# An LSTM recurrence run over 125 lanes in four rounds: a shorter 16-bit rough round, one two-pass round that keeps its sums and states, two rounds of changes, and another order of TensorE's work

## The chip, the cores and the metric

The kernel runs on one core of a Trainium2 chip. The metric is the device time of one execution in microseconds (us).

## The reference, cut to what matters

x has 6250 rows of 512. First a graph layer (a sum over 100,000 edges, two dense layers), then an LSTM over the 6250 rows as one sequence, each with a residual:

```python
x = x + gnn(layernorm(x), edge_index, W1, b1, W2, b2)
def step(carry, x_t):                      # 6250 steps, h and c of 512
    combined = concatenate((x_t, h_prev))
    f_t = sigmoid(combined @ W_f + b_f);  i_t = sigmoid(combined @ W_i + b_i)
    c_tilde = tanh(combined @ W_c + b_c); o_t = sigmoid(combined @ W_o + b_o)
    c_t = f_t * c_prev + i_t * c_tilde;   h_t = o_t * tanh(c_t)
x = x + lstm(layernorm(x), W_f, b_f, W_i, b_i, W_c, b_c, W_o, b_o)
```

## The kernel before, in words

table_part and graph_part compute the graph layer, the rows x1 and, for each of them, the 2048 gate inputs (gate_rows, in DRAM). lstm_part then does the recurrence. It cuts the sequence of 6250 into 125 lanes (L) of 50 steps (STEPS) and runs all lanes side by side, one lane to a partition. A lane's starting state is unknown at first, so it runs in rounds: after each, measure turns the ends of the lanes (cell, product of the forget gates, output gate) by TensorE into columns and takes the gap between a lane's end and the next lane's start, and correct makes new starts from the gaps by a scan with the products (decay). Before, the rounds are rough and close (one pass of rounded weights each), full (three passes: W_high and W_low with the state, W_high with the state's low part; it stores the sums of the gates in total_rows and the turned states in h_steps, both in DRAM) and delta (one pass of W_high with the difference between the new state and the stored one, on top of the stored sums). After full the gaps must be under LOOSE, after delta under TOLERANCE; otherwise rounds "more" (three passes) follow.

The four accumulators acc[n] are one PSUM bank each of 512 columns: n = 0 forget and input gates of the first 256 units, 1 cell and output gates of them, 2 and 3 the same of the second 256 units. product(n, k) is one matmul of 512 columns with the state chunk k (FIRST is k = 0, 1, SECOND is k = 2, 3), 16 in a pass. turn transposes h chunk by chunk into hturn (PSUM); take_turned or moved makes the state of it, and new products wait for it. The rows of a step come by DMA into xg, four buffers deep; they enter the accumulator by a matmul with the identity (add_rows), by a copy into PSUM ahead of the products (seed; seeded is TensorE's wait for it), or, in full, by VectorE's add_inputs into total. Each engine takes its instructions in the order that step writes down for it, and nothing else: in delta, ScalarE has forget_input(0), cell_gate(0), output_gate(0), forget_input(1), new_cell(FIRST) (tanh), cell_gate(1), seed(0), seed(1), output_gate(1), new_cell(SECOND), seed(2), seed(3).

## Time and profile before

| | |
|---|---|
| median of 3 runs | 3029.12 us (3022.49 to 3034.47) |
| profiled execution, span | 3303.4 us; no time of its own is given beside the span |
| granted TensorE clock, mean | 0.938 |
| TensorE busy | 2872.7 us, 87% |
| VectorE busy | 2206.3 us, 67% |
| ScalarE busy | 1745.7 us, 53% |
| GpSimd busy | 996.9 us, 30% |
| DMA | 648.45 MB, 196 GB/s |

The rows shown ahead of the prediction give times from the start of the span. PE is TensorE's matmuls, PEld its weight loads, DVE is VectorE, ACT is ScalarE, POOL is GpSimd. Shares of the whole span are means over stages with different limits, so the stages are to be read one by one.

### The profile page before, as it was taken

What the parts mean: (1) busy time and instruction counts of PE and PEld (TensorE: products, weight loads), DVE (VectorE), ACT (ScalarE), POOL (GpSimd) and SP (SyncE); (2) the same over time, 40 slices, a digit from 0 to 9 for tenths busy, and PEclk for the clock granted to TensorE, in tenths of its full rate; (3) what the DMA queues carried; (4) which work ended last, traced back from release to release, by engine and by line L of the source; (5) the groups of instructions that cost most, each with busy time, mean ns of one, the idle gap of its engine ahead of it and who ended that gap; (6) DMA issues with size and microseconds to landing.
All of it is one profiled execution on the core that took longest, in us unless ns stands there. A gap on an engine that the chain in (4) does not pass through costs nothing. (4 is left out here: it accounts for less than half of the span.)

```text
span 3303.4 us, 57302 instructions
## 1 busy us (share of the span) xinstructions
PE 2872.7 (87%) x11844; PEld 2116.3 (64%) x11845; DVE 2206.3 (67%) x5730; ACT 1745.7 (53%) x4557; POOL 996.9 (30%) x1008
## 2 busy tenths in 40 slices
PE   6967887888887988887869999999999999978786
PEld 5846665666665766665656666666677777755554
DVE  6746776767766766665757886666666666666665
ACT  4644444444444444444437776777344444447775
POOL 1135555555555655555540000000000000003332
PEclk9979988999898999988989999999999999989998
DMA  8556767677776777667666665664466656669997
GB/s 221 159 169 197 204 200 205 200 210 207 209 209 205 212 211 203 205 200 211 191 177 184 183 179 150 171 174 136 138 196 193 194 192 194 194 182 269 260 272 185
DMA packets 234635, 648.45 MB, mean 196 GB/s; under 512 B 65914, under 2 KB 87674, under 8 KB 203334
## 3 DMA queue, kind: packets, MB, share of 16 engines
q1 hardware_dynamic: 161768, 410.64, 42.8%
q0 software_dynamic: 72816, 237.24, 25.1%
q8 instruction: 19, 0.31, 0.0%
q14 instruction: 32, 0.26, 0.0%
HBM read 493.56 MB, written 154.16 MB: 196 GB/s over the span
## 5 line engine op out<-in xcount | busy, mean ns | idle before, releaser
L1474 PE MATMUL acc<-W_high,state 128*125 128x512 f32 x3200 | 998.3, 417 | 43.3 <-ACT acc L1407 38.7
L1474 PEld LDWEIGHTS acc<-W_high,state 128*125 128x125 f32 x3200 | 595.2, 191 | 242.1 <-ACT state L1354 57.1
L785 POOL DMA_INDIRECT rows<-ln_table,slab x400 | 409.5, 1024 | 467.0 <-issue 230.0
L1316 POOL TENSOR_TENSOR out<-h,lx 125x512 f32<-125x512 f32 x50 | 64.2, 1283 | 1394.0 <-DVE h L1753 1394.0
L785 POOL DMA_INDIRECT Wh<-ln_table,slab x400 | 406.1, 1015 | 217.5 <-issue 152.4
L819 ACT ACTIVATE high<-rows 128x512 fp32r<-128x512 f32 x400 | 243.6, 628 | 332.7 <-DMA rows<-ln_table,slab 225.6
L867 PE MATMUL agg<-high,onehot 128*125 128x512 f32 x800 | 347.8, 435 | 52.9 <-DVE low_part L976 38.0
L819 ACT ACTIVATE high<-Wh 128x512 fp32r<-128x512 f32 x400 | 241.3, 629 | 225.2 <-DMA Wh<-ln_table,slab 117.5
L867 PE MATMUL agg<-low_part,onehot 128*125 128x512 f32 x800 | 327.7, 410 | 0.0
L1474 PE MATMUL acc<-W_low,state 128*125 128x512 f32 x800 | 316.3, 395 | 0.0
L1733 DVE TENSOR_TENSOR fc<-gate,c 125x256 f32<-125x256 f32 x400 | 168.7, 422 | 210.4 <-ACT gate L1373 206.5
L976 DVE TENSOR_TENSOR low_part<-rows,high 128x512 fp32r<-128x512 f32 x400 | 261.4, 692 | 70.7 <-ACT high L819 47.3
L976 DVE TENSOR_TENSOR low_part<-Wh,high 128x512 fp32r<-128x512 f32 x400 | 263.9, 690 | 16.3 <-issue 8.0
L1474 PE MATMUL acc<-W_high,h_low 128*125 128x512 f32 x800 | 263.7, 401 | 0.0
L1373 ACT ACTIVATE gate<-acc 125x512 f32<-125x512 f32 x300 | 179.5, 598 | 146.8 <-PE acc L1474 138.7
L1753 DVE TENSOR_TENSOR h<-gate,tc 125x128 f32<-125x128 f32 x800 | 198.5, 288 | 85.6 <-ACT tc L1399 84.9
L1354 ACT ACTIVATE state<-hturn 128x125 fp32r<-128x125 f32 x600 | 140.0, 275 | 187.7 <-PE hturn L1494 181.1
L867 PEld LDWEIGHTS agg<-high,onehot 128*125 128x125 f32 x800 | 157.1, 196 | 123.0 <-issue 52.4
L887 PE MATMUL gps<-Wx_high,zT_high 128*125 128x512 f32 x800 | 221.9, 399 | 14.2 <-ACT zT_high L854 11.9
L913 PE MATMUL late<-W_high,h1T_high 128*125 128x512 f32 x200 | 108.7, 543 | 142.6 <-ACT h1T_high L836 82.5
L1399 ACT ACTIVATE tc<-c 125x128 f32<-125x128 f32 x800 | 203.8, 304 | 53.7 <-DVE c L1745 53.1
L1494 PE MATMUL hturn<-ident,h 125*128 125x125 f32 x800 | 192.2, 295 | 37.3 <-DVE h L1753 37.3
(217 smaller groups left out, 5032.7 us busy)
## 6 DMA issues: line engine op xcount, KB each, us to landing
xg<-gate_rows SPq DMA_DIRECT2D x150, 896.0 KB
gate_rows<-gout SPq DMA_DIRECT2D x200, 224.0 KB
total_rows<-total SPq DMA_DIRECT2D x50, 896.0 KB
xg<-total_rows SPq DMA_DIRECT2D x50, 896.0 KB
xg<-gate_rows SPq DMA_DIRECT2D x150, 104.0 KB
lx<-x_rows POOLq DMA_DIRECT2D x50, 250.0 KB, 8.2
out_dram<-out POOLq DMA_DIRECT2D x50, 250.0 KB, 8.3
h_steps<-hT SPq DMA_DIRECT2D x49, 250.0 KB, 2.6
```

The lines of the kernel that those rows point to most:

```text
L785: e.indirect_dma_start(out=rows[j % RING][:, :], out_offset=None, in_=table[:, :], in_offset=bass.IndirectOffsetOnAxis(ap=slabs[j // SLAB] ...
L819: e.activation(high[j % PARTS][:, :], rows[j % RING][:, :], ACT.Copy).then_inc(s_high, 1)
L867: m = e.matmul(agg[0:L, :], onehot[:, j % HOT_RING, :], part[j % PARTS][:, :], start=(j == 0 and part is high), stop=(part is low_part), s ...
L887: products.append(e.matmul(gps[n][0:L, :], state[:, k, :], weights[:, k, n // 2, n % 2].rearrange("p s c -> p (s c)"), start=(begins and k ...
L976: e.tensor_tensor(low_part[j % PARTS][:, :], rows[j % RING][:, :], high[j % PARTS][:, :].bitcast(F32), ALU.subtract).then_inc(s_low, 1)
L1354: e.activation(state[:, k, :], hturn[k][:, :], ACT.Copy).then_inc(s_state[k], 1)
L1373: e.activation(gate[0:L, half, 0].rearrange("c s u -> c (s u)"), gates, ACT.Sigmoid).then_inc(s_fi[half], 1)
L1399: e.activation(tc[0:L, k], c[0:L, k], ACT.Tanh).then_inc(s_tc[k], 1)
L1474: m = e.matmul(acc[n][0:L, :], stationary[:, k, :], weights[:, k, n // 2, n % 2].rearrange("p s c -> p (s c)"), start=begins, stop=(k == K ...
L1494: e.transpose(hturn[k][:, :], h[par][0:L, k], ident[0:L, 0:L]).then_inc(s_turn[k], 1)
L1733: e.tensor_tensor(fc[0:L, of].rearrange("c k u -> c (k u)"), gate[0:L, half, 0, 0], c[0:L, of].rearrange("c k u -> c (k u)"), ALU.mult).th ...
L1753: e.tensor_tensor(h[par][0:L, k], gate_of(k, 1, 1), tc[0:L, k], ALU.mult).then_inc(s_h[k], 1)
```

## The change

The rounds are now rough, kept, change and final. Rough begins at step SKIP = 12 of each lane (38 steps) with cells, gates and h in 16 bits (fp16, in the memory of total); its turned h is copied into the state by VectorE, no longer ScalarE. Kept has two passes (W_high and W_low with a state that has 16 bits, so there is no low part) and h in 16 bits; its sums go to total_rows as before, its states stay on chip in kept, in the memory in which the weights and some working buffers of the earlier parts were. Change and final are what delta was, against these sums and states, and take their old states from kept instead of a DMA. Only final stores the result. All one-pass rounds share one order of TensorE (one_pass); the seed of accumulator 3 is VectorE's in all of them. fc is gone, the cell is multiplied in place. After kept the gap of the cells counts a quarter, and LOOSE is 2^-3. The diff, cut:

```diff
+SKIP = 12
 TOLERANCE = 2.0 ** -17
-LOOSE = 2.0 ** -7
+LOOSE = 2.0 ** -3
+CELL_SHARE = 0.25
...
+        kept = sb(top, "kept", [P, STEPS, K * LANES], F16)
+        Wh = (kept[:, :, :].rearrange("p t u -> p (t u)")[:, 0:2 * K * G4].bitcast(F32)
+              .rearrange("p (k a b s c) -> p k a b s c", k=K, a=2, b=2, s=2))
+        beside = kept[:, :, :].rearrange("p t u -> p (t u)")[:, 2 * K * G4:].bitcast(I32)
...
+        halves = [t[:, :, :, :].rearrange("p a b g -> p (a b g)").bitcast(F16) for t in total]
+        r_gate = halves[0][:, 0:G4].rearrange("p (a b s u) -> p a b s u", a=2, b=2, s=2)
+        r_c, r_ic, r_tc = (halves[1][:, n * D:(n + 1) * D].rearrange("p (k u) -> p k u", k=K) for n in range(3))
+        r_decay = halves[1][:, 3 * D:4 * D].rearrange("p (a u) -> p a u", a=2)
+        h_half = [t[:, :, :].bitcast(F16)[:, :, 0:P] for t in h]
...
+        hturn = [pb(ctx, f"hturn{k}", [P, P]) for k in range(K)]
+        hturned = [t[:, 0:L] for t in hturn]
+        hturned_half = [t[:, :].bitcast(F16)[:, 0:L] for t in hturn]
...
+        def steps_of_round(e, kind, step):
+
+            begin = SKIP if kind == "rough" else 0
+            step(begin, 0, True, False)
+            with e.Fori(0, (STEPS - 2 - begin) // ROWS) as i:
                 for n in range(ROWS):
-                    step(i * ROWS + (n + 1), (n + 1) % ROWS, False, False)
+                    step(i * ROWS + (begin + n + 1), (n + 1) % ROWS, False, False)
...
+            for r, kind in enumerate(("rough", "kept", "change", "final")):
+                steps(r, kind)
+                measure(r, kind, {"kept": 0, "final": 1}.get(kind))
+                if kind != "final":
+                    correct(r, kind)
...
-            for t in (c, c_start, h_start, gap, h_gap, change):
+            for t in (c, c_start, h_start, gap, h_gap, change, r_c):
                 e.memset(t[:, :, :], 0.0).then_inc(s_clear, 1)
-            e.memset(decay[:, :, :], 1.0).then_inc(s_clear, 1)
+            for t in (decay, r_decay):
...
+                e.memset(t[:, :, :], 1.0).then_inc(s_clear, 1)
+            e.memset(tc_start[:, :, :], 0.0).then_inc(s_clear, 1)
...
                         cell_gate(1)
                         output_gate(1)
+                        new_cell(SECOND)
+                    elif kind == "kept":
+                        if not first:
+                            keep(SECOND, s - 1)
+                        new_cell(FIRST)
+                        forget_input(1)
+                        if not last:
+                            take_turned(FIRST, now)
+                        cell_gate(1)
+                        output_gate(1)
+                        if not last:
+                            keep(FIRST, s)
...
+                    else:
                         forget_input(1)
...
-                        output_gate(1)
-                        if kind == "full" and not last:
-                            keep(FIRST, s, par, summed)
-                    new_cell(SECOND)
-                    if kind == "delta":
+                        new_cell(SECOND)
                         seed(2)
-                        seed(3)
-                    elif last:
-                        take_turned(SECOND, now)
-                steps_of_round(e, step)
+                steps_of_round(e, kind, step)
+                if kind == "kept":
+                    for s in s_state:
+                        e.sem_inc(s, 1)
 
             def correct(r, kind):
                 e.wait_ge(s_cs, r + 1)
@@ -1460,9 +1464,9 @@
         @block.tensor
         def _(e):
             for s in (*s_acc, *s_turn, s_taken):
-                e.sem_inc(s, AHEAD)
...
+                            e.wait_ge(s_seed_v, SEEDED + (s - SKIP))
+                        elif n == 3:
+                            e.wait_ge(s_seed_v, SEEDED + (STEPS - 1 - SKIP) + (r - CHANGE) * (STEPS - 1) + s)
                         else:
...
+                    def one_pass():
+                        if first:
+                            e.wait_ge(s_begin, r + 1)
+                        if first or kind == "rough":
+                            for n in range(4 if first else 3):
+                                m = add_rows(n)
+                            if first:
+                                m.then_inc(s_taken, 1)
+                        if not first:
+                            turn(FIRST, 1 - par, now - 1)
+                        if not first and kind != "rough":
+                            seeded(1)
+                        for n, k in ((0, 0), (1, 0), (0, 1), (1, 1)):
+                            product(n, k)
+                        if kind != "rough":
+                            seeded(2)
+                        for k in FIRST:
+                            product(2, k)
+                        if not first:
+                            turn(SECOND, 1 - par, now - 1)
+                        for n in range(2):
+                            for k in SECOND:
                                 product(n, k)
-
...
                         seeded(3)
...
-                            product(3, k)
-
-                    def close_step():
-                        add_rows(0)
-                        turn(FIRST[:1], 1 - par, now - 1)
-                        add_rows(1)
-                        turn(FIRST[1:], 1 - par, now - 1)
...
+                    def two_passes():
                         if first:
                             e.wait_ge(s_begin, r + 1)
                             e.wait_ge(s_clear, CLEARED + K)
                         for k in FIRST:
                             stated(k)
+                        for n in range(3):
+                            e.wait_ge(s_sum[n], now - 1)
+                            products(n, FIRST, OF_HIGH, True)
+                        if not first:
+                            turn(SECOND, 1 - par, now - 1)
+                        for k in SECOND:
+                            stated(k)
                         for n in range(2):
-                            e.wait_ge(s_sum[n], summed - 1)
+                            products(n, SECOND, OF_HIGH, False).then_inc(s_acc[n], 1)
+                        e.wait_ge(s_sum[3], now - 1)
+                        products(3, FIRST, OF_HIGH, True)
+                        products(2, SECOND, OF_HIGH, False).then_inc(s_acc[2], 1)
+                        products(3, SECOND, OF_HIGH, False).then_inc(s_acc[3], 1)
+                        turn(FIRST, par, now)
...
+                    gates, cell, took, cell_turned, faded = gate, c, ic, tc, decay
+                to_h = h_half if kind in ("rough", "kept") else h
+                if kind == "change":
+                    for k in range(K):
+                        e.wait_ge(s_kept[k], r * STEPS + AHEAD - 1)
+
...
-                            e.tensor_tensor(state[:, k, :], hturn[k][:, :], hT[par][:, k, :],
+                            e.tensor_copy(state[:, k, :], hturned_half[k]).then_inc(s_state[k], 1)
+
+                    def moved(ks):
+                        for k in ks:
+                            e.wait_ge(s_turn[k], now)
+                            e.tensor_tensor(state[:, k, :], hturned[k],
+                                            kept[:, bass.ds(s + 1, 1), k * L:(k + 1) * L]
+                                            .rearrange("p o l -> p (o l)"),
                                             ALU.subtract).then_inc(s_state[k], 1)
...
-                        if kind == "delta" and not last:
-                            moved(FIRST[:1], s, par, now)
+                        if not last:
+                            if kind == "rough":
+                                take_turned(FIRST)
+                            else:
+                                moved(FIRST[:1])
                         for k in SECOND:
                             new_cell(k)
-                        if kind == "delta" and not last:
-                            moved(FIRST[1:], s, par, now)
+                        if not last and kind != "rough":
+                            moved(FIRST[1:])
                         new_h(SECOND)
-                        if kind == "delta":
-                            if not last:
-                                moved(SECOND, s, par, now)
-                        else:
+                        if not last:
+                            if kind == "rough":
+                                take_turned(SECOND)
+                            else:
+                                moved(SECOND)
+                        if kind == "rough":
                             decayed()
-                        if kind == "rough" and not last:
+                        if not last:
                             seed()
+                    elif kind == "kept":
+                        add_inputs(0, landed=True)
+                        add_inputs(1)
+                        forgotten(0)
+                        taken_in(0)
+                        for k in FIRST:
+                            new_cell(k)
+                        add_inputs(2)
+                        new_h(FIRST)
+                        add_inputs(3)
+                        forgotten(1)
+                        taken_in(1)
+                        for k in SECOND:
+                            new_cell(k)
+                        new_h(SECOND)
+                        decayed()
                     else:
                         if not first:
...
+                turned = ends_half if kind == "rough" else ends
...
+                if kind == "rough":
+                    e.wait_ge(s_clear, CLEARED + K)
+                    after_own(e.tensor_copy(begun, h_start[:, :, :]))
+                    after_own(e.tensor_copy(state[:, :, :], begun))
+                elif kind in ("kept", "change"):
+                    after_own(e.tensor_tensor(state[:, :, :], h_start[:, :, :], begun, ALU.subtract))
```

## Rows read from the trace of the kernel before

**Rows 1.** The page: span of the profiled execution

```profile
span 3303.4 us, 57302 instructions
```

**Rows 2.** Windows from each round's first sigmoid: length, busy time of the engines, clock, DMA

```profile
0.00:1714.60 1714.60, 1407.71 (x5831) 1076.79 (x5832) 1148.37 (x2374) 781.50 (x1513) 869.50 (x856) 0.91 0.69 201
1714.60:2021.60 307.00, 291.74 (x1171) 193.67 (x1170) 240.22 (x710) 212.67 (x702) 11.25 (x5) 0.96 0.63 173
2021.60:2339.00 317.40, 303.95 (x1237) 208.68 (x1236) 204.00 (x662) 230.56 (x751) 0.00 (x0) 0.98 0.56 155
2339.00:2951.60 612.60, 596.24 (x2604) 459.22 (x2603) 394.13 (x1173) 261.01 (x898) 0.00 (x0) 0.98 0.60 190
2951.60:3303.40 351.80, 273.11 (x1009) 177.96 (x1007) 219.56 (x811) 259.99 (x696) 116.15 (x148) 0.93 0.90 243
```

**Rows 3.** Once-a-step instructions of rough, close, full and delta: min/median/max ns, first, last

```profile
L1758 DVE TENSOR_TENSOR decay<-decay,gate x48: 681/684/687, 1740.6 to 2005.9; 125x512 f32<-125x512 f32 x48
...
L1758 DVE TENSOR_TENSOR decay<-decay,gate x50: 682/685/690, 2026.6 to 2320.1; 125x512 f32<-125x512 f32 x50
...
L1758 DVE TENSOR_TENSOR decay<-decay,gate x50: 684/685/689, 2346.9 to 2928.4; 125x512 f32<-125x512 f32 x50
...
L1316 POOL TENSOR_TENSOR out<-h,lx x50: 1261/1286/1296, 2956.9 to 3284.7; 125x512 f32<-125x512 f32 x50
```

**Rows 4.** Waits in delta, 2950 to 3280: total us, times, longest

```profile
PEld acc L1474 <- ACT acc L1407: 47.9, 49, 2.6
...
ACT acc L1407 <- DMA xg<-total_rows: 11.8, 14, 1.8
```

**Rows 5.** Timeline of one delta step: start, length, instruction

```profile
3206.66 0.60 ACT L1373 ACTIVATE gate<-acc 125x512 f32<-125x512 f32 x1 [0.72 <-PE acc L1474]
...
3208.05 0.60 ACT L1373 ACTIVATE gate<-acc 125x512 f32<-125x512 f32 x1 [0.23 <-PE acc L1474]
3208.54 0.50 ACT L1399 ACTIVATE tc<-c 125x128 f32<-125x128 f32 x2
3208.97 0.38 ACT L1384 ACTIVATE gate<-acc 125x256 f32<-125x256 f32 x1
3209.25 1.11 ACT L1407 ACTIVATE acc<-xg 125x512 f32<-125x512 f32 x2
...
3210.42 0.95 PE L1474 MATMUL acc<-W_high,state 128*125 128x512 f32 x3 [0.50 <-ACT acc L1407]
...
3210.56 0.51 ACT L1399 ACTIVATE tc<-c 125x128 f32<-125x128 f32 x2
...
3210.95 1.12 ACT L1407 ACTIVATE acc<-xg 125x512 f32<-125x512 f32 x2
...
3211.31 0.53 PE L1494 MATMUL hturn<-ident,h 125*128 125x125 f32 x2
...
3212.79 0.60 ACT L1373 ACTIVATE gate<-acc 125x512 f32<-125x512 f32 x1 [0.72 <-PE acc L1474]
```

**Rows 6.** Timeline of a rough step, second turning

```profile
1859.23 0.40 PE L1494 MATMUL hturn<-ident,h 125*128 125x125 f32 x2
...
1859.86 2.14 PEld L1474 LDWEIGHTS acc<-W_high,state 128*125 128x125 f32 x10 [0.31 <-ACT state L1354]
```

**Rows 7.** Timeline of a full step, TensorE around the second turning

```profile
2464.24 1.09 PE L1474 MATMUL acc<-W_high,h_low 128*125 128x512 f32 x4
...
2466.09 0.38 PE L1494 MATMUL hturn<-ident,h 125*128 125x125 f32 x2
...
2466.98 0.47 PE L1474 MATMUL acc<-W_high,state 128*125 128x512 f32 x1
```

**Rows 8.** Groups by form, 1740 to 2006 and 2345 to 2931: count, busy us, mean ns, idle before

```profile
L1745 DVE TENSOR_TENSOR c<-fc,ic 125x128 f32<-125x128 f32 x188 | 46.5, 289 | 3.2
L1733 DVE TENSOR_TENSOR fc<-gate,c 125x256 f32<-125x256 f32 x94 | 39.7, 422 | 37.8 <-ACT gate L1373 37.8
...
L1709 DVE TENSOR_TENSOR total<-acc,xg 125x512 f32<-125x512 f32 x98 | 67.8, 692 | 77.0 <-PE acc L1474 71.6
```

More of the change, by code:

```diff
@@ L1625, in three_passes, with measure @@
                         if last:
[L1626 to L1628 removed]
+                            turn(SECOND, par, now)
+                    if kind == "kept":
+                        two_passes()
+                    elif kind == "more":
                         three_passes()
[L1630 to L1643 removed]
+                    else:
+                        one_pass()
+                        if last and kind == "final":
+                            turn(range(K), par, now)
+                steps_of_round(e, kind, step)
+                if kind in ("rough", "change"):
+                    for t in s_turn:
+                        e.sem_inc(t, 1)
+            def measure(r, kind, checks):
                 now = (r + 1) * STEPS + AHEAD
```

476 lines of the change are left out of this document (200 added, 276 removed).

## The prediction, made before the changed kernel ran

> **What bounds the kernel now.** I took the profile in the order: span, stages, one step of each round, then the single instructions. The span is 3303.4 us [rows 1], 274 us (9%) above the median of the runs, 3029.12 us, so I work on the profile's own time and carry the difference over at the end. The table of stages [rows 2] has everything ahead of the recurrence in its first row, 1714.6 us; the change moves buffers there and adds no instruction, so that row stays. The other four are the rounds rough, close, full and delta: 307.0, 317.4, 612.6 and 351.8 us. What the reader is to see is how regular they are. In the rough round 48 decay updates start in 265.3 us, 5.645 us a step; close 293.5/49 = 5.99; full 581.5/49 = 11.87; delta 6.13 from one first sigmoid to the next where it runs undisturbed [rows 5], but 327.8 us for its 49 gaps [rows 3], where 49 x 6.13 is 300.4. Those 27 us are late rows: the delta round moves 243 GB/s at a DMA share of 0.90 [rows 2], and there ScalarE waits for xg and TensorE for ScalarE's seeds [rows 4]. What of each row of the table isn't 49 steps is start-up and turnover: 30.4, 23.9, 31.0 and 24.0 us, 109.3 in all.
>
> A step is a ring: accumulators complete, gates, cell, tanh, h, turned h, state, products. In full, TensorE fills it: four products in a row take 1.09 us, three gaps of 0.232 and one latency of 0.39 [rows 7], and 48 x 0.232 = 11.1 of the 11.87. In the one-pass rounds 16 products are 3.7 us, and the ring's latency decides. So halving arithmetic buys little there, and the order in which each engine takes its work buys or costs much.
>
> **Delta step, and the order that change and final get.** Zero is the start of the first sigmoid, 3206.66; the next is at 6.13 [rows 5]. ScalarE's two seeds begin at 2.59 and end at 3.70; the first product starts at 3.76, 0.06 behind. ScalarE's two tanh of the second half start at 3.90 and the next seed, that of accumulator 2, at 4.29. The turning of the second half starts at 4.65, when its h is ready and the next sigmoid comes 1.48 after that turning. ScalarE's order stays the same up to that seed. But TensorE's changes: in one_pass both products of accumulator 2 with the first half stand ahead of turn(SECOND), and they wait for seed 2, which ScalarE does after new_cell(SECOND). An activation of 512 columns lasts 0.60 (the first sigmoid [rows 5]), so seed 2 ends at about 4.88 and TensorE resumes at 4.94; two products (2 x 0.232) put the turning at 5.40 instead of 4.65. Add the 1.48 that follow: 6.88. Between the turning and the sigmoid the old order has one filler product, which waited for nothing, so its removal gives nothing back. Moved reads kept at an address from a register; no row shows one on VectorE, and I take 0.02 (0 to 0.2). So 6.90 a step; the seed of accumulator 3, now on VectorE, is early enough, since four products come ahead of its use. Low bound 6.13 (the wait costs nothing), high 7.2. Two rounds: 98 x 6.90 = 676.2 us, where close and delta had 293.5 and 300.4 + 27.4. Of the 27.4 I leave 2: hT's 256 KB of 1.79 MB a step go in final, in change x1 and y too, and the step is longer.
>
> **Rough, 38 steps.** Old step: second turning at 1859.23, weight load for the next product at 1859.86, 0.63 later [rows 6]; the new order has six products ahead of that turning where the old had four. New chain from the sigmoid: accumulator 2 is complete six products later (1.38), its sigmoid holds ScalarE 0.49 (spacing from the second sigmoid to the tanh behind it, 3208.05 to 3208.54 [rows 5]), tanh of the cells from 1.87, then the cell gate 0.41 later, 2.28 to 2.66 (0.43 behind and 0.38 long in delta [rows 5]); VectorE's ic at 2.70, behind which the copy of the turned h now stands on VectorE: copy at 2.91, product at 3.24. Six products: 4.62; turning to next product 0.63: 5.25; the second behind it 0.33, latency and signal 0.43: 6.01. VectorE then has the decay and the seed of accumulator 3 after the copies of the second half, where they stood before them: that seed is 0.1 to 0.4 late for product(3, 0), which delays accumulators 2 and 3. I take 6.1. What 16 bits give: VectorE's operations on gates and cells. No row shows a 16-bit one. Upper bound: no gain, 422 ns for 256 columns; lower: what half the columns cost, 289 for 128 [rows 8]. I take the lower, but the ring has ScalarE in it at those places, so it gives only room for the copies. With no gain: 6.6; with transposes and copies 0.2 shorter each way: 5.7. ScalarE's times go by columns and stay. So 37 x 6.1 = 225.7 us, against 49 x 5.645 = 276.6. The Trainium skill, "VectorE: DVE Perf Modes", section "What auto-detection actually checks", has tensor_tensor on all-16-bit step-1 operands at two elements a cycle, and operands in PSUM outside the two-port mode; no run here shows it yet. By that rule the sum would be the one I give, by the other 37 x 0.5 = 18 us more.
>
> Three more clears on GpSimd ahead of the round (two of 500 to 512 elements, one more ones-fill) hold the state copy and ScalarE back by some 1.5 us.
>
> **Kept, 50 steps of two passes.** 32 products instead of 48: 7.42 us. This is no longer a step that TensorE fills, since filler is gone. First bubble: turn(SECOND), ScalarE's copies, then products, which wait for both states: 2466.98 - 2466.09 = 0.89 [rows 7]. Second bubble, at turn(FIRST), counted from accumulator 0 complete: accumulator 2 is complete 12 products later (2.78); its sum, put ahead of new_h(FIRST) on VectorE, starts when VectorE is free at 2.87 and holds it 0.61, ends after 0.69 [rows 8] at 3.56; h0 at 3.48 to 3.77, h1 to 3.97, second turning 4.01. ScalarE meanwhile takes forget_input(1) at 3.60 and is free again 0.52 later (two seeds of 512 columns take 1.11, one 0.59 [rows 5]), the two copies end at 4.60, TensorE goes on at 4.68. Its last product of the step began at 3.32 (16 products, less the latency 0.39), so it was free at 3.55: 1.13 idle. Sum 7.42 + 0.89 + 1.13 = 9.44; I take 9.4. Low 8.7 (16-bit transposes and their copies shorter, sums earlier), high 9.8 (a register-addressed copy on ScalarE in the way). 49 x 9.4 = 460.6 against 581.6. Loads and stores are 2.05 MB in 9.4 us, 218 GB/s, under the 243 of delta [rows 2], and a store has two steps to land. The clock: full and rough rounds have 0.98 and 0.96 granted with their turnovers [rows 2], and the rough step has bubbles of 0.6; so I count the upper level, 2.4 GHz, for kept too.
>
> **Sum.** Before: 1714.6 + 276.6 + 293.5 + 581.6 + 300.4 + 27.4 + 109.3 = 3303.4. After: 1714.6 + 225.7 + 460.6 + 676.2 + 2 + 109.3 + 1.5 = 3189.9. The turnovers stay (three corrections and one check after the first two-pass round, as before). That is 114 us less, 3.5%. In parts: rough -51, close replaced by change +45, full replaced by kept -121, delta replaced by final +38 on its steps and -25 in its stalls, +1.5 clears. Carried to the median: in proportion 2925; the 114 us as they are 2915; without the 25 us of stalls, if unprofiled runs had none, 2941. I say 2925 us.
>
> **Rivals.**
> (a) The new order of TensorE costs nothing: if seed 2 were ready before the second half's h, steps stay at 6.13. For: ScalarE has room. Against: the seed's start behind the tanh, in the row. 98 x 0.77 = 75 us less: 3114 of the profile, 2856 in proportion.
> (b) 16 bits give VectorE nothing, and kept runs at its upper bound: 18 + 49 x 0.4 = 38 us more, 2960. For: no row of a 16-bit operation. Against: kept's bubbles are counted from rows.
> (c) Slower, by one mechanism: the last check. If a gap after final is above 2^-17, the kernel goes into a "more" round, three passes of 50 steps, 582 + 31 = 613 us, 3538 us. It decides as soon as one lane misses. For: the rough round is now 38 steps with 16-bit cells, and the looser first check (2^-3) no longer stops a poor start. Against: three corrections lie ahead of the last check as before, and final's differences are taken against states kept to 16 bits, by which a rounded weight errs little.
> (d) No change that can be told: one-pass steps would have to reach about 8.0 us (114/98 more), or kept 11.7. Only with several misses.
>
> **How the numbers follow.** Forecast 0.70, (a) 0.15, (b) 0.07, (c) 0.05, (d) 0.03. The range goes from (a)'s 2850 to 2985: bounds of kept (+20), rough (+18) and one-pass (+29) together added to the forecast without a repeat of the stall; (c) and half of (d) stay out. A difference under 0.5%, some 15 us, can't be told from none in this kernel. Faster 0.91, same 0.03, slower 0.06.
>
> **What would show it.** The stage table: rough near 256 us up to the next round's first sigmoid, kept near 490, change near 360, final near 365. In change, two consecutive first sigmoids 6.9 apart, TensorE idle before product(2, 0) and released by ScalarE's copy into acc. In kept, two idle stretches a step, 0.9 and 1.1 us, released by ScalarE's state copies. No wait for xg in final worth more than a few us. VectorE's 256-column product in rough near 290 ns. Wrong it would be by TensorE's order if that idle stretch is missing, by the last check if instructions of a fifth round appear, and by DMA if change or final show clock drops.

## The result, and the profile after

The changed kernel takes 2934.54 us (median of 4 runs, 2930.0 to 2946.26); beside it the kernel before took 3028.32 us (median of 4, 3022.49 to 3034.47). The ratio is 0.9697, 95% interval 0.9671 to 0.9723: 94 us, 3.0%. The forecast was 2925 us, in the range 2850 to 2985.

The page of the changed kernel, as [rows 1], with the engines' busy time:

```profile
span 2932.2 us, 53818 instructions
...
PE 2515.4 (86%) x10566; PEld 1827.5 (62%) x10567; DVE 2163.7 (74%) x5752; ACT 1600.7 (55%) x4082; POOL 1007.8 (34%) x1011
```

TensorE has 357 us less work than before (2872.7), the span is 371 us shorter than in [rows 1]. Both numbers mislead, and the stages say why. Windows of the changed kernel from the first sigmoid of each round, as [rows 2]: ahead of the recurrence, rough, kept, change, final. Columns: window, length, busy us (and instructions) of PE, PEld, DVE, ACT and POOL, granted clock, DMA share, GB/s.

```profile
0.00:1437.30 1437.30, 1320.24 (x5835) 1036.33 (x5837) 1148.72 (x2375) 764.57 (x1514) 882.57 (x860) 0.97 0.80 240
1437.30:1700.50 263.20, 226.29 (x896) 144.85 (x895) 178.80 (x690) 122.44 (x382) 9.66 (x4) 0.95 0.53 144
1700.50:2193.30 492.80, 428.68 (x1815) 306.89 (x1815) 338.59 (x972) 253.29 (x894) 0.00 (x0) 0.98 0.70 212
2193.30:2559.10 365.80, 272.72 (x1021) 171.45 (x1020) 247.93 (x854) 230.43 (x648) 0.00 (x0) 0.97 0.51 140
2559.10:2932.20 373.10, 267.51 (x1005) 167.97 (x1003) 249.63 (x861) 229.95 (x647) 115.62 (x148) 0.96 0.75 194
```

The first row is 277 us shorter than in [rows 2], though the change neither adds nor removes an instruction there. So I took a second profile of the kernel before, the same file on another occasion; the same windows of it:

```profile
0.00:1437.30 1437.30, 1319.37 (x5830) 1038.33 (x5832) 1147.09 (x2374) 765.62 (x1514) 887.40 (x856) 0.97 0.81 240
1437.30:1743.40 306.10, 291.67 (x1171) 193.88 (x1171) 240.06 (x710) 212.57 (x702) 10.64 (x5) 0.96 0.63 172
1743.40:2060.50 317.10, 303.71 (x1237) 208.78 (x1236) 203.81 (x662) 230.55 (x751) 0.00 (x0) 0.98 0.56 155
2060.50:2672.80 612.30, 595.93 (x2603) 459.07 (x2602) 393.95 (x1173) 260.63 (x897) 0.00 (x0) 0.98 0.61 190
2672.80:3022.20 349.40, 270.27 (x1009) 175.34 (x1007) 219.22 (x811) 260.08 (x696) 116.45 (x148) 0.94 0.90 244
```

Its front is 1437.3 us at 240 GB/s, where the profile that I predicted from had 1714.6 at 201. Its four rounds agree with [rows 2] within 2.4 us each. This is the pair to compare: recurrence 1584.9 before, 1494.9 after, 90 us less; rough -42.9, close to change +48.7, full to kept -119.5, delta to final +23.7.

Instructions that come once a step in the changed kernel, as [rows 3]: ns min/median/max, first and last start. The first is the seed of accumulator 3 in rough, the second the decay update in kept, the last two the seed in change and in final.

```profile
L1785 DVE COPY acc<-xg x37: 687/687/689, 1451.5 to 1680.2; 125x512 f32<-125x512 f32 x37
...
L1779 DVE TENSOR_TENSOR decay<-decay,gate x50: 684/685/689, 1706.0 to 2170.9; 125x512 f32<-125x512 f32 x50
...
L1785 DVE COPY acc<-xg x49: 683/684/686, 2199.4 to 2539.2; 125x512 f32<-125x512 f32 x49
...
L1785 DVE COPY acc<-xg x49: 683/684/686, 2565.3 to 2907.8; 125x512 f32<-125x512 f32 x49
```

228.7/36 is 6.35 us a rough step, 464.9/49 is 9.49 a kept one, 339.8/48 and 342.5/48 are 7.08 and 7.14 in change and final. The median step of the last two is 7.00, from one first sigmoid to the next; the rest is a few long steps, of which more below.

**One step of change**, as [rows 5]: start, length, instruction, idle before it.

```profile
2320.42 0.60 ACT L1374 ACTIVATE gate<-acc 125x512 f32<-125x512 f32 x1 [2.15 <-PE acc L1478]
...
2324.14 1.92 PE L1478 MATMUL acc<-W_high,state 128*125 128x512 f32 x6 [0.49 <-ACT acc L1408]
...
2324.27 0.52 ACT L1400 ACTIVATE tc<-c 125x128 f32<-125x128 f32 x2
2324.67 0.61 ACT L1408 ACTIVATE acc<-xg 125x512 f32<-125x512 f32 x1
2324.68 0.49 DVE L1774 TENSOR_TENSOR h<-gate,tc 125x128 f32<-125x128 f32 x2 [0.19 <-ACT tc L1400]
2325.33 0.29 PEld L1478 LDWEIGHTS acc<-W_high,state 128*125 128x125 f32 x2 [0.43 <-ACT acc L1408]
...
2325.89 0.38 PE L1500 MATMUL hturn<-ident,h 125*128 125x125 f32 x2
2326.31 0.48 DVE L1749 TENSOR_TENSOR state<-hturn,kept 128x125 fp32r<-128x125 f32 x2 [1.13 <-PE hturn L1500]
...
2327.41 0.60 ACT L1374 ACTIVATE gate<-acc 125x512 f32<-125x512 f32 x1 [2.13 <-PE acc L1478]
```

The reader is to see the weight load at 2325.33 and what stands behind it. h of the second half begins on VectorE at 2324.68. TensorE can't turn it, because product(2, 0) stands ahead and waits for ScalarE's seed of accumulator 2, 2324.67 to 2325.28. TensorE resumes 0.05 later, does its two products, and turns at 2325.89, 5.47 from the first sigmoid; in [rows 5] that was 4.65. The h of the second half was complete at 2325.17 (2324.68 + 0.49), so the turning waited for its place in TensorE's order and not for h. The group of six products in the row hides this: two of its six stand behind the wait.

The waits of change, 2200 to 2540 (us in all, times, longest), as [rows 4]:

```profile
PEld acc L1478 <- ACT acc L1408: 53.0, 96, 0.7
```

TensorE waits for ScalarE's seeds twice a step (96 times), where delta had it once [rows 4], and nothing waits for xg.

**One rough step and one kept step** of the changed kernel, timeline rows as [rows 6, 7]:

```profile
1560.29 0.60 ACT L1374 ACTIVATE total<-acc 125x512 f16<-125x512 f32 x1 [2.06 <-PE acc L1478]
1560.66 1.22 PEld L1478 LDWEIGHTS acc<-W_high,state 128*125 128x125 f32 x6 [0.38 <-DVE acc L1785]
...
1565.23 0.29 PE L1498 MATMUL hturn<-ident_h,h 125*128 125x125 f16 x2
...
1565.84 1.19 PE L1478 MATMUL acc<-W_high,state 128*125 128x512 f32 x4 [0.32 <-DVE state L1744]
...
1566.60 0.60 ACT L1374 ACTIVATE total<-acc 125x512 f16<-125x512 f32 x1 [2.06 <-PE acc L1478]
...
1940.08 0.40 PE L1478 MATMUL acc<-W_low,state 128*125 128x512 f32 x1
...
1940.32 0.63 ACT L1374 ACTIVATE gate<-total 125x512 f32<-125x512 f32 x1 [0.29 <-DVE total L1728]
...
1940.86 0.43 ACT L1356 ACTIVATE state<-hturn 128x125 fp32r<-128x125 f16 x2
...
1941.39 0.47 PE L1478 MATMUL acc<-W_high,state 128*125 128x512 f32 x1 [0.41 <-ACT state L1356]
...
1944.25 0.28 PE L1498 MATMUL hturn<-ident_h,h 125*128 125x125 f16 x2
...
1945.11 0.47 PE L1478 MATMUL acc<-W_high,state 128*125 128x512 f32 x1 [0.57 <-ACT state L1356]
```

In rough, TensorE's weight load waits 0.38 for the seed of accumulator 3, which VectorE does last in its step; the products themselves lose half of that, two of their spacings being 0.33 instead of 0.23 us. In kept, TensorE's last product of a step starts at 1940.08 and would let the next start 0.232 later; it starts at 1941.39, so 1.08 goes, with ScalarE's sigmoid (1940.32) between the turning and its copies; behind the second turning, 1944.25, it is 0.86. One more thing can be read from such rows: the first product behind an idle stretch is followed by the next one 0.30 to 0.33 later, not 0.232. So four products in a row take 1.19 at 1565.84, where the four of [rows 7] take 1.09.

VectorE's groups of the rough round (count, busy us, mean ns, idle before), as [rows 8]:

```profile
L1744 DVE CAST state<-hturn 128x125 fp32r<-128x125 f16 x136 | 32.6, 282 | 21.3 <-PE hturn L1498 21.3
...
L1756 DVE TENSOR_TENSOR total<-total 125x256 f16<-125x256 f16 x68 | 19.9, 293 | 32.3 <-ACT total L1374 32.3
...
L1779 DVE TENSOR_TENSOR total<-total 125x512 f16<-125x512 f16 x34 | 14.1, 416 | 0.0
```

256 columns of 16 bits take 293 ns against 422 [rows 8], 512 take 416 against 685 [rows 3]: about the price of half the columns. The copy out of PSUM, 282 ns for 125 columns, is no faster than a 32-bit operation on 128 (289 [rows 8]). The Trainium skill, "VectorE: DVE Perf Modes", section "What auto-detection actually checks", has tensor_tensor at the doubled rate where every operand is 16-bit with step 1, which these operations are and the copy, with its 32-bit result, is not; this trace agrees.

### The profile page after: what moved, and what is told of

Read it like the earlier page. It is cut to its first block, busy times and chain, and to the rows that moved or that the text cites. A ratio compares the mean times of both kernels' runs of the same rounds, so it can differ in the third digit from the quotient of the medians.

```text
span 2932.2 us, 53818 instructions
## 1 busy us (share of the span) xinstructions
PE 2515.4 (86%) x10566; PEld 1827.5 (62%) x10567; DVE 2163.7 (74%) x5752; ACT 1600.7 (55%) x4082; POOL 1007.8 (34%) x1011
## 4 chain that ended last, share of the span: by engine, by line
PE 29%; ACT 10%; DVE 9%; issue 2%; POOL 0%; DVEq 0%; ACTq 0%; POOLq 0%
PE acc L1478 28%; ACT acc L1408 3%; ACT gate L1374 3%; DVE total L1728 1%; DVE state L1749 1%; ACT state L1356 1%; ACT gate L1385 1%; ACT tc L1400 1%; DVE c L1766 1%; ACT total L1374 1%; DVE ic L1761 1%; DVE total L1730 1%; DVE state L1744 1%; DVE total L1732 1%; DVE h L1774 1%
## 5 line engine op out<-in xcount | busy, mean ns | idle before, releaser
L790 POOL DMA_INDIRECT kept<-ln_table,slab x800 | 826.1, 1033 | 385.8 <-issue 227.3
L824 ACT ACTIVATE high<-kept 128x512 fp32r<-128x512 f32 x800 | 471.3, 628 | 345.9 <-DMA kept<-ln_table,slab 259.9
L981 DVE TENSOR_TENSOR low_part<-kept,high 128x512 fp32r<-128x512 f32 x800 | 523.2, 693 | 30.1 <-ACT high L824 24.0
L892 PE MATMUL gps<-Wx_low,zT_high 128*125 128x512 f32 x800 | 216.2, 392 | 0.0
L892 PE MATMUL gps<-Wx_high,zT_low 128*125 128x512 f32 x800 | 207.9, 392 | 0.0
L872 PEld LDWEIGHTS agg<-low_part,onehot 128*125 128x125 f32 x800 | 152.6, 191 | 32.1
L892 PEld LDWEIGHTS gps<-Wx_high,zT_high 128*125 128x125 f32 x800 | 148.1, 185 | 38.4 <-issue 1.0
L1774 DVE TENSOR_TENSOR h<-gate,tc 125x128 f32<-125x128 f32 (+1 forms) x600 | 148.5, 288 | 31.2 <-ACT tc L1400 30.5
L892 PEld LDWEIGHTS gps<-Wx_low,zT_high 128*125 128x125 f32 x800 | 148.2, 185 | 36.2
L1478 PEld LDWEIGHTS acc<-W_low,state 128*125 128x125 f32 x800 | 149.6, 187 | 32.3
```

Source lines behind the costliest of these rows:

```text
L790: e.indirect_dma_start(out=rows[j % RING][:, :], out_offset=None, in_=table[:, :], in_offset=bass.IndirectOffsetOnAxis(ap=slabs[j // SLAB] ...
L824: e.activation(high[j % PARTS][:, :], rows[j % RING][:, :], ACT.Copy).then_inc(s_high, 1)
L872: m = e.matmul(agg[0:L, :], onehot[:, j % HOT_RING, :], part[j % PARTS][:, :], start=(j == 0 and part is high), stop=(part is low_part), s ...
L892: products.append(e.matmul(gps[n][0:L, :], state[:, k, :], weights[:, k, n // 2, n % 2].rearrange("p s c -> p (s c)"), start=(begins and k ...
L981: e.tensor_tensor(low_part[j % PARTS][:, :], rows[j % RING][:, :], high[j % PARTS][:, :].bitcast(F32), ALU.subtract).then_inc(s_low, 1)
L1478: m = e.matmul(acc[n][0:L, :], stationary[:, k, :], weights[:, k, n // 2, n % 2].rearrange("p s c -> p (s c)"), start=begins, stop=(k == K ...
```

## The experiments

My theory: a step is a ring of latencies, and what each engine's order puts between an h and its turning, or between a turning and its copy, sets the time. Rival: TensorE's, VectorE's and ScalarE's work itself, or the transfers, set it, and a changed order alone moves nothing.

**The turning ahead of accumulator 2, in change and final.**

```diff
+                        if not first and kind != "rough":
+                            turn(SECOND, 1 - par, now - 1)
                         if kind != "rough":
                             seeded(2)
                         for k in FIRST:
                             product(2, k)
-                        if not first:
+                        if not first and not (kind != "rough"):
                             turn(SECOND, 1 - par, now - 1)
```

> The changed kernel, but in change and final turn(SECOND) stands ahead of the wait for seed 2 and the products of accumulator 2. Theory (the turning of the second half waits behind a seed that ScalarE does after its last tanh): steps fall from 7.00 to about 6.15, 98 x 0.85 = 83 us less, 2850 us, less some late rows in final, which then needs 250 GB/s. Rival (VectorE's longer queue, with the third seed and the read of kept at a register's address, makes the step longer): steps stay above 6.8, at most 20 us less. The granted clock, which falls for 3.4 us every 80 to 90 us in these rounds, should no longer do so if it follows from TensorE's idle stretches of 7.00 us steps (some 10 us more).

2862.94 us (4 runs, 2860.73 to 2870.52), ratio 0.9483 (0.9448 to 0.9518). A step is 6.28 instead of 7.00 (five of the other kernels below leave change and final as they are, and have a median of 7.00 or 7.01 in both). One step of change in this kernel:

```profile
2328.08 1.21 PE L1478 MATMUL acc<-W_high,state 128*125 128x512 f32 x4 [0.49 <-ACT acc L1408]
...
2328.61 0.61 ACT L1408 ACTIVATE acc<-xg 125x512 f32<-125x512 f32 x1
...
2329.13 0.38 PE L1500 MATMUL hturn<-ident,h 125*128 125x125 f32 x2
...
2330.65 0.60 ACT L1374 ACTIVATE gate<-acc 125x512 f32<-125x512 f32 x1 [1.44 <-PE acc L1478]
```

Four products, then the turning, 0.09 before the seed of accumulator 2 has ended. No instruction was taken away and none made faster, and the 49 gaps of the two rounds went from 346.7 and 349.4 us to 309.4 and 310.6, 76 less. The rival is out for these two rounds.

**The same wait, from ScalarE's side:** its seed ahead of its tanh.

```diff
                         output_gate(1)
+                        seed(2)
                         new_cell(SECOND)
-                        seed(2)
```

> The changed kernel, but ScalarE copies seed 2 ahead of new_cell(SECOND) in change and final; TensorE's order is kept. Theory: TensorE no longer waits for seed 2, but both tanh and so h of the second half come 0.53 us later, so the second turning goes from 5.5 to about 5.2 after the first sigmoid, steps about 6.7, 98 x 0.3 = 29 us less, 2905 us. Rival (the wait for the seed is all there is): steps 6.2 as with the turning moved, 2855 us.

2904.88 us (2 runs), ratio 0.9613 (0.9571 to 0.9656), 6.73 a step. TensorE no longer waits for seed 2, but h of the second half comes later by the seed, 4.78 behind the first sigmoid instead of 4.26: the tanh begins at 2323.64, behind the seed of 0.61:

```profile
2323.11 0.61 ACT L1408 ACTIVATE acc<-xg 125x512 f32<-125x512 f32 x1
...
2323.64 0.51 ACT L1400 ACTIVATE tc<-c 125x128 f32<-125x128 f32 x2
```

So the wait can be moved between the engines but is only gone when the turning goes first.

**The turning first in rough alone** (the condition of the first diff is `kind == "rough"`).

> The changed kernel, but in rough turn(SECOND) stands ahead of the two products of accumulator 2. Theory (six products ahead of the turning instead of four cost 0.46, less what the h of the second half isn't ready): steps from 6.33 to 5.95, 37 x 0.38 = 14 us less. Rival (rough is set by ScalarE and VectorE, whose order changed too): steps stay at 6.3.

2920.95 us (2 runs), ratio 0.9666 (0.9622 to 0.9711). Rough 5.89 a step, 226.4 us for its 37 gaps, against 6.34 and 243.3.

**The seed of accumulator 3 ahead of the decay, in rough.**

```diff
+                        if not last:
+                            seed()
                         if kind == "rough":
                             decayed()
-                        if not last:
-                            seed()
```

> The changed kernel, but in rough VectorE makes the seed of accumulator 3 ahead of the decay. Theory (that seed is late for product(3, 0) and delays accumulators 2 and 3): the seed comes 0.33 earlier, the sum of waits in a step falls by about 0.2, steps from 6.33 to 6.1, 9 us less. Rival (the seed is in time): steps stay at 6.33.

2934.44 us (2 runs) beside 3021.31, ratio 0.9706 (0.9648 to 0.9763): the total can't tell it. Its own round does: 6.16 a step, 236.0 us, 7 less.

**In kept, h ahead of the sum on VectorE, the copies ahead of a sigmoid on ScalarE.**

```diff
                         new_cell(FIRST)
-                        forget_input(1)
                         if not last:
                             take_turned(FIRST, now)
+                        forget_input(1)
                         cell_gate(1)
...
+                        new_h(FIRST)
                         add_inputs(2)
-                        new_h(FIRST)
                         add_inputs(3)
```

> The changed kernel, but in kept VectorE makes h of the first half ahead of the sum of accumulator 2, and ScalarE takes the turned first half ahead of forget_input(1). Theory (the second idle stretch of TensorE, 1.1 us, comes from these two orders): h0 and h1 come 0.35 us earlier and the copies 0.3 us, steps from 9.49 to 9.2, 14 us less. Rival (the turning waits for its place behind the products of accumulator 3): steps stay at 9.4 or more.

2926.13 us (2 runs), ratio 0.9678 (0.9628 to 0.9728); the total alone wouldn't show it. Kept is 9.23 a step, 452.1 us against 464.9. ScalarE in this kernel:

```profile
1941.49 0.44 ACT L1356 ACTIVATE state<-hturn 128x125 fp32r<-128x125 f16 x2 [0.56 <-PE hturn L1498]
1941.97 0.63 ACT L1374 ACTIVATE gate<-total 125x512 f32<-125x512 f32 x1
```

The copies now wait for the turning, not for ScalarE.

**The rough round in 32 bits.** Gates, cells, products and tanh are 32-bit again; h and its turning stay at 16 bits. The rounding of this round is changed by it.

```diff
+        clear_c, clear_decay = r_c, r_decay
+        r_gate, r_c, r_ic, r_tc, r_decay = gate, c, ic, tc, decay
         h_half = [t[:, :, :].bitcast(F16)[:, :, 0:P] for t in h]
...
```

> The changed kernel, but in rough the gates, cells, decay and tanh are in 32 bits (h and its turning stay in 16). Theory: VectorE's operations there last 0.42, 0.29 and 0.69 us instead of 0.29, 0.22 and 0.42; the copies of the turned h and the seed come later, steps from 6.33 to about 6.6, 10 us more. Rival (the ring has ScalarE in it at those places and 16 bits give nothing): steps stay at 6.35.

2953.05 us (2 runs), ratio 0.9767 (0.9731 to 0.9804). Rough 6.80 a step, 260.3 us: 17 us more. VectorE's 256-column product is back at its old length:

```profile
L1758 DVE TENSOR_TENSOR c<-gate,c 125x256 f32<-125x256 f32 x63 | 26.8, 426 | 19.5 <-ACT gate L1376 15.6
```

So 16 bits are worth 0.46 a step, and the order of TensorE (6.34 - 5.89) 0.45: in this round the change gave with one hand and took with the other. A step of the changed rough round is longer than the 5.645 of before [rows 3], 16 bits and all, so what the round saves it saves by its 12 skipped steps. With turning and seed first it is 5.73 (below), still not under 5.645; no run moves the copies of the turned h back to ScalarE, so their share isn't known.

**A shorter rough round** (26 steps instead of 38, so the later rounds start from poorer states).

```diff
-SKIP = 12
+SKIP = 24
```

> The changed kernel, but the rough round begins at step 24 of each lane, so it has 26 steps instead of 38. It prices the skipped steps and asks how near the last check is. If the gaps still pass: 12 x 6.33 = 76 us less, 2858 us, all else the same. If they don't, a fifth round of three passes runs: 610 us more than that, about 3470 us. I give the first 0.6.

3875.13 us (2 runs), ratio 1.2817 (1.2768 to 1.2866). One of the two checks of the gaps isn't met and a fifth round runs, the outcome to which I had given 0.4. The kernel joins both checks, the one behind kept (LOOSE) and the one behind final (TOLERANCE), into one value behind final, so the trace doesn't tell which. Windows of it, and of what follows it:

```profile
2864.80:3450.60 585.80, 582.59 (x2570) 452.87 (x2569) 379.37 (x1138) 226.16 (x695) 128.49 (x146) 1.00 0.44 125
3450.60:3872.20 421.60, 3.92 (x19) 2.72 (x19) 14.03 (x37) 2.28 (x7) 2.09 (x2) 0.51 0.00 1
```

The round costs 586 us, where I had 613. The second row wasn't in the prediction: 422 us in which next to nothing runs. The further rounds stand in a loop of MORE = 250 passes, and a pass that isn't needed still tests and skips on every engine, 421.6/249, 1.7 us each. In sum 1007 us. When both checks are met, none of this is paid: the span then ends with final.

**All of the better orders** (turning first in all one-pass rounds, seed ahead of decay, kept's h and copies first).

> The changed kernel with four orders changed together: the second turning ahead of the wait for seed 2 and the products of accumulator 2 in rough, change and final, the seed ahead of the decay in rough, and kept's h of the first half ahead of the sum of accumulator 2. Theory (each edit acts in its own round): the rounds shorten by what the single runs showed, 37 and 39 us for change and final, 17 and a few more for rough, 13 for kept, together 110 us, 2825 us. Rival (they meet in the transfers or in the clock): less than 90 us, over 2845 us.

2826.25 us (median of 5, 2822.47 to 2828.62) beside 3024.28, ratio 0.9338 (0.9311 to 0.9365). Steps: 5.73, 9.23, 6.28, 6.29. This beats both kernels, by 3.6 points over the change as it was made. The recurrence:

```profile
1440.70:2827.00 1386.30, 1138.86 (x4732) 790.99 (x4731) 1021.75 (x3377) 837.01 (x2569) 126.22 (x152) 0.97 0.69 192
```

**Accumulator 2 as a whole behind 0 and 1.** Built on the last one: in change and final four products, the turning, (0,2), (0,3), (1,2), (1,3), then seeded(2) and all of accumulator 2, to win the last 0.15 back to 6.13.

```diff
+                        if not first:
+                            turn(SECOND, 1 - par, now - 1)
+                        if kind in ("change", "final"):
+                            for n in range(2):
+                                for k in SECOND:
+                                    product(n, k)
+                            seeded(2)
+                            for k in range(K):
+                                product(2, k)
+                            seeded(3)
...
```

> As the run with four orders, but in change and final TensorE has accumulators 0 and 1 complete before it waits for seed 2, then all of accumulator 2, then 3, which is the order of the delta round of the kernel before. Theory (6.28 instead of 6.13 comes from the two products between the turning and the products of the second half, held up by seed 2): steps 6.13, 98 x 0.15 = 15 us less, 2810 us. Rival (VectorE's seed of accumulator 3 and the read at a register's address make the 0.15): steps stay at 6.28. Final then moves 1.54 MB in 6.13 us, 250 GB/s, so some late rows may come back and take 5 to 10 us of it.

2840.20 us (5 runs, 2836.93 to 2844.56), ratio 0.9384 (0.9357 to 0.9411): slower than the last one by 14 us, where I expected 15 us less. The step is 6.32. The two products in question had held the next one back by only 0.03, and without them that one stands behind an idle stretch and costs as much more; what is left is that h of the second half comes 0.04 later. In change the clock fell ten times for 3.4 us, and the 49 gaps of that round take 325.0 us against 310.5.

**The same with SKIP = 16**, 34 rough steps.

> As the last, but the rough round begins at step 16, so it has 34 steps. With 24 skipped the last check failed once and cost a fifth round of 613 us and about 420 us more for the loop around it. If it passes with 16: 4 x 5.8 = 23 us less than the run before. If not: about 1030 us more.

3825.42 us (2 runs), ratio 1.2644. A fifth round again. So both checks are met at 38 rough steps and not at 34, in this kernel and for these inputs; the margin against rival (c) is under four steps.

**Delta's order to the letter**, on top of the one with accumulator 2 last: (1,0), (0,0), (0,1), the turning, (1,1) and the rest.

```diff
-                        for n, k in ((0, 0), (1, 0), (0, 1), (1, 1)):
+                        early = ((1, 0), (0, 0), (0, 1)) if kind in ("change", "final") else ((0, 0), (1, 0), (0, 1), (1, 1))
+                        for n, k in early:
                             product(n, k)
-                        if kind != "rough":
+                        if not first:
+                            turn(SECOND, 1 - par, now - 1)
+                        if kind in ("change", "final"):
+                            product(1, 1)
...
```

> As the last run but one (38 rough steps), with the order of the old delta round to the letter in change and final: three products ahead of the second turning, the fourth behind it. Theory (the fourth product ahead of the turning holds it back 0.1, and it fills the time of VectorE's difference otherwise): steps from 6.32 to 6.15, 17 us less, 2825 us. Rival (VectorE's read of kept at an address from registers, or its seed, makes the step longer than delta's 6.13): steps stay at 6.25 or more. The granted clock fell ten times in change in the run before, some 15 us; if that follows from how TensorE's work is spread, it stays, and the time is 2825 to 2835.

3118.21 us (4 runs, 3104.24 to 3129.22), but the kernel before takes 3328.1 us there (7 runs, 3308.49 to 3348.35), ratio 0.9383 (0.9328 to 0.9437). Two windows: ahead of the recurrence and behind:

```profile
0.00:1727.10 1727.10, 1414.00 (x5834) 1070.49 (x5836) 1147.91 (x2375) 784.67 (x1513) 893.86 (x860) 0.91 0.69 200
1727.10:3102.60 1375.50, 1166.08 (x4733) 790.05 (x4731) 1021.45 (x3377) 842.23 (x2569) 125.17 (x152) 0.98 0.68 193
```

This chip has the slow front of [rows 2], and the kernel before is some 300 us slower on it too, so the ratio isn't to be set beside that of the better orders. Its recurrence is the shortest of all, 1375.5 us, 11 less than with all the better orders. Its steps are 6.23, where I expected 6.15 and the rival had 6.25 or more: against the 6.32 of the kernel that it is built on that is 0.09, from the turning behind three products rather than four, and 0.10 is left to delta's 6.13. One delta step of the kernel before, then one step of change in this one:

```profile
3211.68 0.49 DVE L1727 TENSOR_TENSOR state<-hturn,hT 128x125 fp32r<-128x125 f32 x2 [0.22 <-PE hturn L1494]
```

```profile
2457.66 0.53 PE L1500 MATMUL hturn<-ident,h 125*128 125x125 f32 x2
...
2458.13 0.49 DVE L1764 TENSOR_TENSOR state<-hturn,kept 128x125 fp32r<-128x125 f32 x2 [0.33 <-PE hturn L1500]
```

The turning is the same in both, 0.53 long and 4.65 behind the first sigmoid. VectorE's difference starts 0.37 behind it in delta (3211.68 less the 3211.31 of [rows 5]) and 0.47 here. So the last 0.10 stands in the start of the difference whose second operand is now read from kept.

## Why the prediction was right, and what in it was not

**Direction and mechanism held.** The sum gave the recurrence 1475 us after the change (3189.9 - 1714.6); 1494.9 was measured, 20 more. By its terms: steps of rough +9, of kept +4, of change and final +10, long steps +8, turnovers -11. One by one:

- Change and final, 6.90 predicted, 7.00 measured. The seed of accumulator 2 was to end at 4.88 and did at 4.86; TensorE was to resume at 4.94 and did at 4.91; the turning was to start at 5.40 and started at 5.47, and the sigmoid came 1.52 behind it, not 1.48. The turning put first, as the mechanism asks, takes 0.72 off the step. Two terms were too small. The two products ahead of the turning were counted 0.232 each, but the first product behind an idle stretch holds the next back 0.33; the 0.10 was there to be read, in the three products of [rows 5] that take 0.95 and not 0.85. And the moved read, put at 0.02 without a row, costs 0.11: VectorE's difference starts 0.15 behind the end of the turning in the changed kernel, 0.04 behind it in delta; the copies in rough, which read no kept, also start 0.04 behind. Here a shorter turning (0.27 instead of 0.33 each, its weights being loaded early) hides half of that. What in the moved read costs the time, its address from a register or its 16-bit operand, no run separates. 98 x 0.10 = 9.8 us.
- Long steps in the same rounds: 346.7 and 349.4 us for 49 gaps, where 49 x 7.00 is 343.0, so 10 us, where the sum had 2. Here a reading was wrong. The prediction put all of delta's 27 us down to late rows, but its own row has only 11.8 us of waits for xg [rows 4], and in that profile the clock fell ten times in delta, each fall worth some 1.3 us (an estimate from the long steps of the changed kernel). The late rows did go: no wait for xg remains. The clock falls stayed, seven of them, and they are the 10 us. The prediction named clock falls in change or final as the sign that DMA had it wrong; the sign appeared, and no transfer was late.
- Rough, 6.1 predicted, 6.34 measured: 37 x 0.24 = 9 us. (The 243.3 us from first to last sigmoid hold a first gap of 15.15, as the round before the change had one of 15.39; like there it counts as turnover.) The seed of accumulator 3 was named as late by 0.1 to 0.4, but only 0.09 of it was put into the step; put first it gives 0.18. Of the 0.15 between 6.16 and 6.01, 0.10 is again the first of the six products behind an idle stretch, counted 0.232 and not 0.34. The price of 16 bits was right: without them 6.6 expected and 6.80 measured, 17 us for the round against 18.
- Kept, 9.4 predicted, 9.49 measured: 464.9 us against 460.6. Its two idle stretches are 1.08 (1.13) and, behind the second turning, 0.86 (0.89). With 7.42 that makes 9.36; the rest is the first product behind each stretch, 0.07 over the usual spacing (0.30 instead of 0.232). The 2.05 MB a step cost nothing that can be seen: no wait for a transfer.
- Turnovers, 109.3 + 1.5 us predicted: 99 measured, which is 1494.9 less 37 x 6.34, 49 x 9.49, 98 x 7.00 and the 10 us of long steps. By rounds, window less steps, they are 28.6, 27.8, 19.1 and 23.7, where the kernel before had 30.4 (rough), 31.0 (full), 23.9 (close) and 24.0 (delta) us; the largest part of the 11 us is behind change. What made them shorter stays open.
- Carrying over to the median. In proportion gave 2925, the 114 us as they are 2915. Neither was right in kind: the 281 us by which that profile's span lies above the second one's are all but 4 in the front, which the change doesn't touch. Two errors met here. The absolute carrying was the better founded, and with 90 measured in place of 114 it gives 2939, 5 us from the result; the proportional one shrank a saving that had no reason to shrink, and so hid part of the miss. That 2925 came out nearer to 2934.54 than 2915 is luck. (The 114 us are 3.4% of 3303.4, not 3.5.)

**Rivals.** (a), the order costs nothing: false, as its price came to 0.72 of the 0.77 a step, and the kernel with the turning first takes 2863 us against (a)'s 2856. (b), 16 bits give nothing and kept is at its upper bound: false, 17 us, and 9.49 against 9.8. (c), a check isn't met: didn't occur, but its price was wrong. The 613 us are 27 more than the round took, and they leave out the loop around it, which makes it 1007. At the chance of 0.05 this changes no forecast, but a reader who weighs a shorter rough round must know it. (d): false.

**Open.** Which of the two checks misses with 34 and with 26 rough steps. What in the moved read makes VectorE's difference start 0.11 later. Why a rough step, in 16 bits and with the better orders, is still no shorter than the 32-bit one of before. And what sets the clock falls.

## What to carry to other kernels

Where a step is a ring and engines take their work in a fixed order, price an order by writing down for each engine what stands ahead of the instruction that the ring waits for; here three such places were worth 108 us, more than the 94 us of the change itself, which among other things took a third of the products out of a round. Count the first product behind an idle stretch by its own row, not by the spacing of the others. Compare stages before totals: a front that differs by 277 us between two executions of one file says nothing of a change behind it, and a saving made elsewhere is then carried as it is. Before idle time is put down to one cause, add up the waits that name it; here they came to 11.8 of 27 us. Price a rare path by running it once, with the loop that stands around it.

## What the runs showed of the hardware that I had not expected

TensorE's clock fell to its lower level, 1.2 GHz, in the middle of regular steps, with no transfer late. In change (the fall, and 14 us to either side):

```profile
2261.00:2275.40 14.40, 10.86 (x43) 6.92 (x43) 9.77 (x34) 9.24 (x26) 0.00 (x0) 1.00 0.55 150
2275.40:2278.80 3.40, 3.12 (x9) 2.14 (x8) 1.37 (x4) 0.66 (x2) 0.00 (x0) 0.51 0.12 27
2278.80:2293.00 14.20, 10.68 (x42) 6.72 (x42) 9.58 (x34) 9.27 (x27) 0.00 (x0) 1.00 0.55 144
```

Ahead of it TensorE is busy 10.86 of 14.40 us, as it is throughout. There were 7 such falls in change and final, most 72 to 92 us apart, each of which makes two steps together some 1.3 us longer. The same two rounds had 2 falls with the turning first, none with the seed early, 3 with all the better orders, 1 with delta's order, and 12 with accumulator 2 last, ten of them in change, mostly 20.5 us apart. Delta itself had 10 in the first profile of the kernel before and 8 in the second, where I had put all of its lost time down to late rows. TensorE's busy share doesn't tell these kernels apart: it is 0.75 in the changed kernel and 0.75 with the seed early, with 7 falls and with none. These counts are of one execution each; five kernels that leave change and final as they are have 7 or 8 falls there. So an order of instructions can cost time by a way that its own ring doesn't show; why one order falls often and its neighbour doesn't stays open.

The front of the kernel took 1437 to 1451 us on most occasions, at 240 GB/s, and 1715 and 1727 us on two, at about 200, with the same instructions. The transfers themselves were not slower: the DMA engines were busy 0.81 of 1437.3 and 0.69 of 1714.6 us, 1164 and 1183 us, nearly the same time, so on the slow occasions they stood idle more. Why stays open. And the loop's empty passes, at 1.7 us each, were dearer than I would have put a test and a branch.
